# The last edge stage of a graph network: ring of three batches, small steps between chunk steps

## The reference

```
h = x @ W
a_src = h @ att_src
a_dst = h @ att_dst
e = leaky_relu(a_src[src] + a_dst[dst], 0.2)
m = segment_max(e, dst, N)
e = exp(e - m[dst])
denom = segment_sum(e, dst, N)
alpha = e / (denom[dst] + 1e-16)
out = segment_sum(h[src] * alpha[:, None], dst, N)
x = layernorm(x + tanh(out + bias))
```

## Time and profile before

| | us |
|---|---|
| median of three runs | 11399.82 |
| lowest and highest | 11399.76, 11401.9 |
| the profiled execution | 11406.15 |
| its span, first to last instruction | 11404.3 |
| first gather of the stage begins | 9256.24 |
| last gather of the stage begins | 11279.92 |
| last `e_out` of the stage ends | 11304.08 |
| first gather of the last node stage begins | 11309.17 |

### The profile page before, as it was taken

The page is one execution under the profiler, slowest core; times in us unless marked ns, Lnnn a source line. Parts: engine busy times, 40 slices in busy tenths (PEclk is TensorE's granted clock), DMA queues, the critical chain, the costliest instruction groups (busy, mean ns, idle before and its releaser), DMA issues. The chain is left out here.

```text
span 11404.3 us, 81326 instructions
## 1 busy us (share of the span) xinstructions
PE 4465.4 (39%) x15877; PEld 3003.7 (26%) x15877; DVE 6589.5 (58%) x11020; ACT 1415.8 (12%) x3304; POOL 8115.1 (71%) x8559
## 2 busy tenths in 40 slices
PE   3167666663222222243232323332323234444443
PEld 3066656662111111121111111111111123333332
DVE  9966666666555555555555555555555555555555
ACT  3011111111000000010000000000000023333333
POOL 2177777776777777757777776777777777777776
PEclk8555555555555555565555555555555555555665
DMA  3177788774333333323333333333333323333332
GB/s 96 57 200 206 205 203 205 205 204 124 98 99 98 99 99 98 91 71 98 100 98 99 98 100 80 98 99 99 98 99 98 95 60 81 82 82 81 81 83 68
DMA packets 1061469, 1264.91 MB, mean 111 GB/s; under 512 B 489075, under 2 KB 841315, under 8 KB 1060611
## 3 DMA queue, kind: packets, MB, share of 16 engines
q0 software_dynamic: 303968, 521.40, 20.5%
q1 hardware_dynamic: 638571, 636.33, 17.4%
q10 hardware_dynamic: 118432, 101.99, 3.6%
HBM read 830.35 MB, written 428.44 MB: 110 GB/s over the span
## 5 line engine op out<-in xcount | busy, mean ns | idle before, releaser
L825 POOL DMA_INDIRECT e_got<-kv_tab,dst_cols x1664 | 1584.1, 952 | 518.1 <-issue 507.3
L1106 POOL DMA_INDIRECT e2a_got<-x_tab,src_cols x1616 | 1524.8, 944 | 566.6 <-issue 566.6
L1763 POOL DMA_INDIRECT e_got<-h_tab,src_tcols x1616 | 1532.4, 948 | 502.5 <-issue 502.5
L1106 POOL DMA_INDIRECT e2b_got<-x_tab,src_cols x1616 | 1524.8, 944 | 512.0 <-issue 512.0
L1106 POOL DMA_INDIRECT e_got<-x_tab,src_cols x1616 | 1524.7, 944 | 507.3 <-issue 507.3
L835 PE MATMUL e_Q<-e_window,e_pick 128*128 128x96 f32 x3328 | 797.3, 418 | 696.9 <-issue 442.5
L1122 PE MATMUL e_EA<-we_We,e_attr 128*128 128x384 f32 x808 | 577.4, 870 | 1072.3 <-DVE e_emsg L1141 1072.3
L1122 PE MATMUL e2a_EA<-we_W_edge,e2a_attr 128*128 128x384 f32 x808 | 579.9, 873 | 1056.5 <-DVE e2a_emsg L1141 1056.5
L1122 PE MATMUL e2b_EA<-we_W_edge,e2b_attr 128*128 128x384 f32 x808 | 581.0, 874 | 1051.7 <-DVE e2b_emsg L1141 1051.7
L835 PEld LDWEIGHTS e_Q<-e_window,e_pick 128*128 128x128 f32 x3328 | 713.9, 317 | 803.2 <-issue 600.2
L1141 DVE TENSOR_TENSOR e2b_emsg<-e2b_EA,e2b_got 128x768 f32<-128x768 f32 x202 | 192.9, 955 | 728.4 <-issue 711.5
(11 more groups left out here) (368 smaller groups left out, 10371.3 us busy)
## 6 DMA issues: line engine op xcount, KB each, us to landing
scan_out<-e_out SPq DMA_DIRECT2D x416, 200.0 KB
e_window<-q_tab SPq DMA_DIRECT2D x1664, 48.0 KB
scan_out<-e_out SPq DMA_DIRECT2D x404, 196.0 KB
scan_out<-e_out SPq DMA_DIRECT2D x202, 384.0 KB
scan_out<-e2a_out SPq DMA_DIRECT2D x202, 384.0 KB
scan_out<-e2b_out SPq DMA_DIRECT2D x202, 384.0 KB
e_rel<-rel_row ACTq DMA_DIRECT2D x416, 128.0 KB
e_keep<-keep_row ACTq DMA_DIRECT2D x416, 100.0 KB
```

The lines of the kernel that those rows point to most:

```text
L825: e.indirect_dma_start(got[u][:, k, :], None, kv_tab, bass.IndirectOffsetOnAxis(dst_c[:, c * K + k:c * K + k + 1], axis=0)).then_inc(s_g[u ...
L1106: e.indirect_dma_start(got[s % RS][:, k, :], None, x_tab, bass.IndirectOffsetOnAxis(src_cols[:, q:q + 1], axis=0)).then_inc(edge_got[s % R ...
L1763: e.indirect_dma_start(got[c % RG][:, k, :], None, h_tab, bass.IndirectOffsetOnAxis(src_tcols[:, q:q + 1], axis=0)).then_inc(s_g[c % RG], 16)
```

## The change

- The ring `got` now holds RB = 3 batches, 48 tiles. There is no `hold` and no copy into it: TensorE's `scores` and VectorE's product read `got` directly. GpSimd asks, at the start of a chunk, whether the product of the chunk twelve before has been made (`v_add`).
- `WT` is a part of the PSUM tile `small`; ACT copies it once a batch to `wts` in SBUF (two of them), and VectorE's copy and product read `wts`.
- The small steps are four pieces on VectorE (`logits`, `carries`, `maxima`, `factors`) and five on TensorE, and one piece follows each chunk step of the batch before.
- The scan of a chunk now follows the product of the chunk two after it (one before). `emsg`, `msg`, `run`, `Z` have three buffers, `parts`, `ad_t`, `neg_t` two.
- ACT copies the message of chunk c - 1 and the output of chunk c - 4 at position c. SP loads `ad_t` and `neg_t` a batch ahead and stores the batch before last.
- 1612 tiles are gathered; the four tiles that hold padding alone are left out, and the last batch waits for 12.

```diff
-            got = [ph.sb(f"got{u}", [P, K, HW]) for u in range(RG)]
-            hold = ph.sb("hold", [P, BT, HW])
+            got = ph.sb("got", [P, RB * BT, HW])
...
+            wts = [ph.sb(f"wts{i}", [P, 2 * BT]) for i in range(2)]
+            TILES = -(-n_edges // P)
...
-                    for c in range(NCH):
-                        if c >= RG:
-                            H.wait(e, f"hold{(c - RG) % U}", (c - RG) // U)
-                        for k in range(K):
-                            q = c * K + k
-                            e.indirect_dma_start(got[c % RG][:, k, :], None, h_tab, bass.IndirectOffsetOnAxis(src_tcols[:, q:q + 1], axis=0)).then_inc(s_g[c % RG], 16)
+                    for q in range(TILES):
+                        it, c = q // BT, q // K
+                        if q % K == 0:
+                            after(e, v_add, c - RB * U + 1)
+                        e.indirect_dma_start(got[:, q % (RB * BT), :], None, h_tab, bass.IndirectOffsetOnAxis(src_tcols[:, q:q + 1], axis=0)).then_inc(s_g[it % RB], 16)
...
+                    for it in range(1, NI + 1):
+                        c = (it - 1) * U
+                        more = it < NI
+                        if more:
+                            scores(it)
+                        spread(c)
+                        forward(c)
+                        if c > 1:
+                            turn_back(c - 2)
+                        if more:
+                            last(it)
+                        spread(c + 1)
+                        forward(c + 1)
+                        if c > 1:
+                            turn_back(c - 1)
+                        if more:
+                            carried_in(it)
+                        spread(c + 2)
+                        forward(c + 2)
+                        turn_back(c)
+                        if more:
+                            tops(it)
+                        spread(c + 3)
+                        forward(c + 3)
+                        if more:
+                            weights(it)
+                        turn_back(c + 1)
+                    turn_back(NCH - 2)
+                    turn_back(NCH - 1)
...
-                        V[u].give(e.tensor_copy(emsg[u % 2][:, :, DN], WT[:, BT + u * K:BT + (u + 1) * K]), "top")
-                        V[u].give(e.tensor_tensor(emsg[u % 2][:, :, 0:DN], hold[:, u * K:(u + 1) * K, 0:DN],
-                                                  WT[:, u * K:(u + 1) * K].unsqueeze(2).to_broadcast([P, K, DN]), ALU.mult), "add")
+                        w = wts[it % 2]
+                        e.tensor_copy(emsg[c % 3][:, :, DN], w[:, BT + u * K:BT + (u + 1) * K])
+                        e.tensor_tensor(emsg[c % 3][:, :, 0:DN], got[:, at:at + K, 0:DN],
+                                        w[:, u * K:(u + 1) * K].unsqueeze(2).to_broadcast([P, K, DN]), ALU.mult).then_inc(v_add, 1)
...
+                    batch = (logits, carries, maxima, factors)
+                    for it in range(NI + 1):
+                        for u in range(U):
+                            c = (it - 1) * U + u
+                            if it > 0:
+                                add(c)
+                                if c > 1:
+                                    scan(c - 2)
+                            if it < NI:
+                                batch[u](it)
+                    scan(NCH - 2)
+                    scan(NCH - 1)
...
-                            H.give(e.activation(hold[:, u * K:(u + 1) * K, :], got[c % RG][:, :, :], ACT.Copy), f"hold{u}")
...
+                        if it < NI:
+                            TB.wait(e, "weights", it)
+                            e.activation(wts[it % 2][:, :], WT, ACT.Copy).then_inc(a_wt, 1)
```

## The result

The changed kernel takes 11498.7 us (median of 4 runs, 11495.2 to 11508.5); the kernel before, on the same chip, 11400.1 us. The ratio is 1.0087, interval [1.0075, 1.0099]: slower by 99 us where 13 us were predicted, and outside the range of 11393 to 11437. The profiled execution took 11508.49 us around a span of 11506.6.

A forecast was written before the change was run, and what follows sets the result against it. The prediction took GpSimd's back-to-back gathers as the bound. Ends and count, -4.3 us, plus longer gathers, +17 us, gave +13 us on 11399.8: 11413 us, range 11393 to 11437.

The forecast's parts named there:

- What bounds the kernel: Steady part of the stage: GpSimd's back-to-back gathers set the time, 1.2485 us each, 19.98 us a batch; everything else waits.
- Fewer gathers, faster landing, longer tail: Stage's end: last scores start 7.9 us earlier, including 5.0 for four gathers; tail 3.6 us longer; together -4.3 us.
- ACT's copies, the ring, the new waits at nothing: Steady part: dropping 404 ACT copies gains nothing, and the new waits of GpSimd and SP cost nothing.
- What a gather costs: Gathers delayed by VectorE operations with two SBUF inputs: 0.17 us a batch, 17 us in all.
- the walk: VectorE's operations in one batch, timed from the scores' start (t = 0) against gather starts at 1.25, 2.50 and on.
- nothing held: Rival: no gather is prolonged by a VectorE operation; -4.3 us, 11395.5 us; chance 0.26.
- several operations hold: Rival: several VectorE operations a batch prolong gathers, 0.35 to 0.52 us a batch, net +31 to +48 us; chance 0.24.

The follow-up runs named there:

- e1: The kernel before, with the four tiles that hold padding alone not gathered; 11402.4 us, ratio 0.9995.
- e9: The kernel before, with the padding slots fetching rows of different nodes instead of one row; 11396.0 us in one run.
- e4: e5 with the copy and product of one chunk in four, the one behind `own`, reading weights in PSUM; 11458.7 us, ratio 1.0052.
- e6: e5 with only the product of the chunk behind `own` reading weights in PSUM, its copy still from SBUF; 11462.8 us, ratio 1.0054.
- e7: The kernel before, with the weights copied to SBUF once a batch and read there by copies and products; 11443.5 us, ratio 1.0039.
- e3: The changed kernel, with the copy and product behind `own` waiting until `opened` has ended; 11416.7 us, ratio 1.0008.
- e2: e5 with all products and copies reading the weights in PSUM, without ACT's copy to SBUF; 11415.3 us, ratio 1.0007.
- e8: e2 with the scores after the leaky step also in PSUM, so `own` and `rm` have one SBUF input; 11398.3 us, ratio 0.9998.
- e5: The control: the changed kernel with `WT` in its own PSUM bank, two `Z` buffers for three, `tops` after `forward`; 11529.6 us, ratio 1.0107.
- e10: e1 with the padding slots of its last tile naming different rows; 11396.8 us, ratio 0.9995.

## Why the prediction was wrong, step by step

- **What bounds the kernel**: right. The gathers' count times their length, plus the ends, gives the result to 1 us: +107.9 - 5.0 - 0.5 (ends) = +102.4 against 11508.49 - 11406.15 = 102.3 for the two profiled executions (the medians differ by 98.7).
- **Fewer gathers, faster landing, longer tail**: right, and confirmed apart by e1 and e9. The scores after the last gather 3.04 us for 3.2, the tail 20.96 for 21.6. Predicted -4.3 us for ends and count; from these rows -5.0 - 0.5 = -5.5.
- **ACT's copies, the ring, the new waits at nothing**: right. ACT lost 213 us and nothing came of it. POOL's idle time per gather is unchanged, though the releaser named before 78 of them is now the product's semaphore (23.8 us, 0.30 each, the usual time of a gather's issue).
- **What a gather costs**: this term failed, +17 us predicted and 107.9 measured. Around `own` the walk was right. It had `own` begin 0.13 us before a gather and end at 1.53, the first product from 1.70 to 2.25, a gap of 0.17; the batch at 10318 has 0.13 and 0.17. What failed is the price: "`own` crosses 1.25 and ends 0.28 behind it: 0.16 us", and with it "nothing when it begins after the gather". Each operation was priced alone, by its own end. Priced by the end of the product it closes up with, the same walk gives 2.25 + 0.82 - 1.25 - 0.94 = 0.88 us; the gather of 10318.15 has 1.82 - 0.94 = 0.88. Gathers behind the batch's first product, 80 in 101 batches, make 68.2 us of the 107.9.
- The rest of the term is phase and small margins. With `own` at 0.88 us the later gathers stand elsewhere than the walk had them, and behind the third product, which missed there, 99 gathers are long (15.0 us). The fourth product "begins 0.09 after 9.99 and misses": in the runs, products that begin 0.03 to 0.10 us after a gather hold it (85 of 85 at 0.08 or 0.09 in e4, 86 of 86 at 0.08 to 0.10 in e6, 47 of 47 at 0.03 or 0.04 in e7), and those 0.11 to 0.14 us after it don't (0 of 55 in e7, 0 of 86 in e3).
- `rm` was cleared by a misreading of the earlier trace rows. The scan of 9005.24 held nothing, and the prediction laid that to its first value, which is read from a tensor. But its input `F` lies in PSUM (`F = [ph.ps(...)]` in the kernel before), so it has one SBUF input, and the row said nothing on `rm`, which has two. `rm` did hold in 81 batches, 13.5 us.
- **The rule of the Trainium skill** (SBUF — State Buffer, section "Who interferes with whom"), by which a `tensor_tensor` with two SBUF inputs doesn't stall descriptor generation, stood behind part of the 0.26 given to "nothing held". Its first half, that a DVE instruction with two SBUF inputs contends with a GpSimd instruction that reads SBUF, fits e2 and e8 (120.3 us in the control, 19.6, then 7.1); the gathers read their row numbers from SBUF. Its inference about descriptor generation is refuted by the same runs: the gathers do wait.
- **The chances**: "several operations hold" was the right rival, at 0.24, and its price of 0.35 to 0.52 us a batch had the same fault. The most the prediction would grant, 0.52 us a batch, came from phase alone; the true 1.07 (107.9 / 101) lay outside every case. From rows that all showed one isolated operation no bound above for several in a row should have been taken.

## What to carry to other kernels

When GpSimd's indirect DMAs bound a stage, an edit that takes load off every other engine can still lose, if it turns a PSUM operand of a frequent DVE operation into an SBUF one. Count the operations with two SBUF inputs that can run as a gather begins, and for each ask what follows it: a large product that closes up with it can add its own length to the hold, as here behind `own`, though small operations that followed `rm` at once added nothing. The loss is gone when the products, `own` and `rm` each have one input in PSUM (e8), and nearly so when a gap, here of 0.36 us, stands between `own` and the product (e3). Since each hold shifts the phase of all that come after, judge by the summed length of the gathers, not by one row.

## What the runs showed of the hardware

- **Two outcomes behind `own`, 0.03 us apart.** In the changed kernel 79 gathers behind `own` had the product 0.17 or 0.18 us after `own`'s end: all ended 0.82 or 0.83 us behind the product's end. In 16 the gap was 0.20 or 0.21: all ended 1.04 or 1.05 behind `own`'s end, which is 0.83 to 0.84 behind the product's *start*. The first rows above show one of each (products of 10297.50 and 10318.60). In e5 it was 53 and 33, with the same numbers. The whole difference of the gap is the copy between them: it begins 0.10 or 0.11 us after `own` ends in both cases and takes 0.18 us in the second, 0.15 in the first. So the gap may be an effect of who got through first and not the cause; that isn't settled. Only the gap of 0.36 was set by an edit (e3), and there the gather follows `own` by 0.76.
- **Not every close row is a chain.** Behind `rm` a `z` with two SBUF inputs (16x128) begins 0.03 or 0.04 us after its end (10323.17 above), then both `wd`, then the product. Still all 120 gathers held by `rm`, 81 of them in the changed kernel, ended 0.75 to 0.77 us behind `rm`. And in e5 this gather takes 0.94 us, though three operations with two SBUF inputs follow each other without a gap:

```profile
10318.52 0.27 DVE L1912 TENSOR_TENSOR e_wd<-e_zl,e_rm 16x128 f32<-16x128 f32 x1
...
10318.68 0.94 POOL L1753 DMA_INDIRECT e_got<-h_tab,src_tcols  x1 [0.30 <-issue]
10318.73 0.27 DVE L1914 TENSOR_TENSOR e_wd<-e_z,e_rm 16x128 f32<-16x128 f32 x1
...
10319.00 0.54 DVE L1884 TENSOR_TENSOR e_emsg<-e_got,e_wts 128x388 f32<-128x388 f32 x1
```

The same holds for 204 gathers in e4, e5 and e6. In all of them the first operation ends 0.11 to 0.13 us after the gather's start, too early to cost anything by itself (0.12 + 0.82 = 0.94), and the second begins 0.04 to 0.06 after that start. Only the product is seen to carry a hold on: behind `own`, and twice behind the second `wd` (gathers of 1.52 us in e4 and 1.53 in e6, 0.82 behind the product). What sets it apart stays open.
- **When an operation must begin to hold a gather.** `own` held a gather when its lead, the time by which it began before the gather, was at least 0.05 us, with one exception at 0.05 (e4). With leads of 0 to 0.04 the gather took 0.94 or 0.95 in 37 of 38 cases of six kernels (once 1.13, in e3). `rm` needed more: it held from a lead of 0.11 us on, and with leads of 0.01 to 0.10 none of 301 gathers (all kernels but e8). Products held when they began up to 0.10 us after the gather. It isn't scan against product: the second `wd`, no scan, also of 16x128, held at leads of 0.06 to 0.12 (seven gathers) and none of the 207 gathers that had begun 0.04 to 0.06 us before it. Why the products differ stays open.
- **One SBUF input isn't always free.** A cast from SBUF to SBUF, the first of the `parts` (16x128, 0.19 us), held 85 gathers in e3 and 22 in e2: they ended 0.82 or 0.83 us behind it. It cost 0.05 us each at most, since the cast is short. Where the cast began level with the gather and the gather wasn't held, the cast took 0.25 or 0.26 us instead (all 99 in the changed kernel): then VectorE pays.
- **One row fetched 128 times lands in 5.6 us, 128 different rows in 2.6** (e9, one execution; 2.45 us in e10), with the gather itself at 0.94 us on POOL either way.
